# Last attention stage: another order of VectorE's work from the middle of a group

## The reference

```python
h = jnp.maximum(_layernorm(x, axis=-1), 0.0)
x = x + _L3_gnn_ref(h, adj, Wq, Wk, Wv, bv, Wo, bo)

# _L3_gnn_ref, 12 heads of 32
q = (x @ Wq.T).reshape(B, N, NUM_HEADS, HEAD)
k = (x @ Wk.T).reshape(B, N, NUM_HEADS, HEAD)
v = (x @ Wv.T + bv).reshape(B, N, NUM_HEADS, HEAD)
a = jnp.einsum('bnhd,bmhd->bhnm', q, k) * SCALE + encoding_bias[:, None, :, :]
pad_mask = jnp.all(a == 0, axis=-1)
a = jnp.where(pad_mask[..., None], -jnp.inf, a)
a = jax.nn.softmax(a, axis=-1)
a = jnp.nan_to_num(a)
o = jnp.einsum('bhnm,bmhd->bnhd', a, v).reshape(B, N, HIDDEN)
return o @ Wo.T + bo
```

## Time and profile before

| what | value |
|---|---|
| median of three runs | 2923.13 us (2920.32 to 2926.05) |
| the profiled execution | 2924.59 us, its span 2922.8 us |
| PE busy | 2767.9 us, 95% of the span |
| DVE busy | 1962.4 us, 67% |
| ACT busy | 1035.7 us, 35% |
| POOL busy | 961.9 us, 33% |
| mean granted clock of TensorE | 0.991 |
| L675 (PE, a projection by rows) | 1103.7 us busy, 60.4 us idle before it |
| chain that ended last | PE 72%, DVE 15%, issue 6%, POOL 4%, ACT 2% |

### The profile page before, as it was taken

How to read it: one execution, slowest core, us unless ns; L and a number is a source line. 1 busy time by engine, 2 the same in 40 slices (tenths; PEclk the granted TensorE clock), 3 DMA queues, 4 the chain that set the end, 5 groups by cost and what they waited for, 6 DMA issues and landing times.

```text
span 2922.8 us, 64340 instructions
## 1 busy us (share of the span) xinstructions
PE 2767.9 (95%) x26048; PEld 2337.1 (80%) x26048; DVE 1962.4 (67%) x4550; ACT 1035.7 (35%) x1985; POOL 961.9 (33%) x874
## 2 busy tenths in 40 slices
PE   6999999999989999999999999999998899999997
PEld 5888888888878888887888888888887777877776
DVE  4455445555567677778777776777777777777775
ACT  2333333333334444444333332222222344433342
POOL 1222113444443333333111110334344344444443
PEclk9999999999999999999999999999999999999999
DMA  3222332333421211221222223222332111111101
GB/s 95 69 69 76 100 106 83 99 109 109 128 70 36 72 48 49 72 73 57 71 71 71 61 88 111 70 92 81 103 103 86 37 36 49 48 48 48 36 26 36
DMA packets 197320, 211.45 MB, mean 72 GB/s; under 512 B 72736, under 2 KB 197024, under 8 KB 197024
## 3 DMA queue, kind: packets, MB, share of 16 engines
q1 hardware_dynamic: 197024, 207.33, 23.1%
HBM read 131.80 MB, written 75.50 MB: 71 GB/s over the span
## 4 chain that ended last, share of the span: by engine, by line
PE 72%; DVE 15%; issue 6%; POOL 4%; ACT 2%; DMA 1%; SPq 0%; DVEq 0%; POOLq 0%; ACTq 0%
PE psum L672 27%; PE psum L675 25%; DVE v_x L1504 4%; PE psum L723 3%; PE psum L990 3%; PE psum L660 2%; PE psum L840 2%; PE psum L885 2%; PE psum L829 2%; DVE room L1535 2%; PE psum L975 2%; PE psum L739 2%; POOL room L507 1%; POOL room L505 1%; PE psum L861 1%
## 5 line engine op out<-in xcount | busy, mean ns | idle before, releaser
L675 PE MATMUL psum<-fast 128*128 128x384 f32 x5760 | 1103.7, 343 | 60.4 <-DVE v_x L1504 28.1
L675 PEld LDWEIGHTS psum<-fast 128*128 128x128 f32 x5760 | 994.7, 189 | 129.6 <-DVE v_x L1504 39.3
L672 PE MATMUL psum<-fast 128*128 128x512 f32 x3456 | 861.7, 400 | 11.4 <-ACT room L1191 4.9
L672 PEld LDWEIGHTS psum<-fast 128*128 128x128 f32 x3456 | 637.1, 189 | 166.8 <-issue 22.7
L526 POOL TENSOR_TENSOR room<-room 128x768 f32<-128x768 f32 x128 | 188.8, 1475 | 418.4 <-DVE room L1541 260.2
L1642 DVE TENSOR_TENSOR room<-psum,rows 128x384 f32<-128x384 f32 x384 | 212.2, 553 | 120.4 <-PE psum L675 119.8
L1135 ACT ACTIVATE room<-psum 128x512 f32<-128x512 f32 x192 | 114.7, 597 | 391.3 <-PE psum L672 391.3
L660 PE MATMUL psum<-mask,z_sb 128*128 128x128 f32 x1152 | 177.7, 285 | 55.1 <-ACT z_sb L1116 21.9
L1116 ACT ACTIVATE z_sb<-x_ring,negb,rstd 128x384 f32<-128x384 f32 x256 | 168.0, 701 | 119.4 <-DVE negb L1367 119.4
L1504 DVE TENSOR_TENSOR v_x<-psum,rows 64x192 f32<-64x192 f32 x512 | 181.4, 354 | 27.9 <-PE psum L675 22.6
L660 PEld LDWEIGHTS psum<-mask,z_sb 128*128 128x128 f32 x1152 | 130.4, 143 | 85.9 <-issue 32.7
(11 more groups left out here) (96 smaller groups left out, 3575.0 us busy)
## 6 DMA issues: line engine op xcount, KB each, us to landing
x_ring<-x_mid SPq DMA_DIRECT2D x64, 768.0 KB, 4.6
x_mid<-x_ring SPq DMA_DIRECT2D x48, 768.0 KB, 4.0
x_ring<-x_in SPq DMA_DIRECT2D x32, 768.0 KB, 4.7
z_mid<-x_ring SPq DMA_DIRECT2D x32, 768.0 KB, 4.1
z_sb<-z_mid SPq DMA_DIRECT2D x32, 768.0 KB, 6.5
out<-x_ring SPq DMA_DIRECT2D x16, 768.0 KB, 3.9
w_raw<-w_all SPq DMA_DIRECT2D x19, 576.0 KB, 7.1
adjc<-adj SPq DMA_DIRECT2D x64, 128.0 KB, 3.9
```

The costliest lines, as they stand in the source:

```text
L672: mm = nc.tensor.matmul(dst, wpart[s_][:, c, c_out * P:(c_out + 1) * P], hpart[:, c, 0:GT], start=(k == 0), stop=(k == 3 * C - 1))
L675: mm = nc.tensor.matmul(dst[:, 0:H], hpart[:, c, row:row + P], wpart[s_][:, c, :], start=(k == 0), stop=(k == 3 * C - 1))
```

## The change

In `a_body` on VectorE, from `nat(0)` on, the last stage (`g.third`) gets an order of its own. `a_add_x` t1 stands ahead of `a_sums` t3; the value copies `nat` t1, the output rows `a_keep_o` t2 and the low part `low` 2 stand ahead of the scores' bias and maxima of the next group's t0 (`a_soft(F, 0)`); `a_sums(F, 0)` goes behind `a_keep_o` t3, and `a_soft(F, 1)` behind `nat` t3. The other attention stage takes the `else` branch, which has its old order. No instruction is added or removed, and no other engine's list changes.

```diff
--- before.py
+++ after.py
@@ -1611,23 +1611,36 @@
                 next_w(F, X, 1)
                 low(0)
                 nat(0)
-                a_sums(g, 3)
-                a_add_x(g, 1)
-                low(1)
-                if F:
-                    a_soft(F, 0)
-                nat(1)
-                a_keep_o(g, 2)
-                low(2)
-                if F:
-                    a_sums(F, 0)
-                nat(2)
-                if F:
-                    a_soft(F, 1)
-                a_add_x(g, 2)
-                a_keep_o(g, 3)
-                nat(3)
-                a_add_x(g, 3)
+                if g.third:
+                    a_add_x(g, 1)
+                    a_sums(g, 3)
+                    low(1)
+                    nat(1)
+                    a_keep_o(g, 2)
+                    low(2)
+                    if F:
+                        a_soft(F, 0)
+                    nat(2)
+                    a_add_x(g, 2)
+                    a_keep_o(g, 3)
+                    if F:
+                        a_sums(F, 0)
+                    nat(3)
+                    if F:
+                        a_soft(F, 1)
+                    a_add_x(g, 3)
+                else:
+                    low(1)
+                    if F:
+                        a_soft(F, 0)
+                    nat(1)
+                    a_keep_o(g, 2)
+                    low(2)
+                    nat(2)
+                    if F:
+                        a_soft(F, 1)
+                    a_keep_o(g, 3)
+                    nat(3)
 
             def c_nat(G, i):
```

## The result

The changed kernel takes 2995.78 us (median of four runs, 2990.58 to 2996.69), the kernel before 2924.47 (four runs, 2920.32 to 2926.05). The ratio is 1.0241, with a 95% interval of 1.0229 to 1.0254: slower, by 71 us. The forecast was 2985, the range 2964 to 3006.

The account below looks back on a forecast made before the run. TensorE bounds the last stage and VectorE causes all its waits. First body 0.5, thirteen full bodies 53.3, fifteenth 2.7 and last 5.1 add 61.6 us to the profiled 2924.6: 2986, forecast 2985 us, range 2964 to 3006.

Parts of the forecast that it names:

- The waits at parts 7 and 8 go, a wait at mix t3 comes: TensorE, last stage: waits of 0.54 and 1.21 us go; late first scores bring 2.3 us at mix t3.
- The residual add of t3 waits for GpSimd behind the second scores: End of VectorE's body: second scores six microseconds late, VectorE idle 2.7 us before this add, TensorE's part 1 waits 2.4.
- The loop: Ring of steps from one `a_soft(F, 1)` to the next: 44.04 us against 39.92, 4.1 us more per full body.
- The smaller waits: TensorE's idle time besides part 1 and mix t3: about 1.4 us at turn t1, the rest at the next body's first turn.
- The clock: Rival: TensorE's clock falls in many bodies, 2.6 us each; 3019 us in all, 3002 in half of them; chance 0.12.
- The first body: First body the change meets in the last stage: costs 0.5 us net.
- the fifteenth: Body without statistics or norms: pays only part 1 (2.4) and its own mix (0.3), 2.7 us.
- The last body: VectorE starts 5.1 us late, had 0.95 of pause, sums of t3 stand 0.9 later: costs 5.1 us.
- only mix t3 changes hands: Rival: VectorE's pauses swallow the second scores' lateness, each body costs 0.5 us, 2931 us; chance 0.07.
- faster: Rival: TensorE loses waits at parts 7 and 8, nobody misses the scores; 24 us gained, 2899 us; chance 0.04.

Follow-up runs that it names:

- The new end alone: Kernel before with only the end of VectorE's order changed (sums of next t0 and second scores later), old middle kept: 2976.30 us, ratio 1.0193.
- The early bias: Changed kernel with GpSimd's output bias of t3 ahead of the next group's weighing and second subtraction: 2969.90 us, ratio 1.0169 to the kernel before.
- The filled kernel: Changed kernel with TensorE's scores of t2 made three times and out t2 twice, same results: 2983.76 us, ratio 1.0210 to the kernel before.
- the middle alone: VectorE's middle as changed, but second scores ahead of the sums, output rows and value copy of t3: 2938.05 us, ratio 1.0062 to the kernel before.
- the kernel with both cures: Changed kernel with GpSimd's early bias of t3 and ScalarE's copy of turn t3's second half ahead of the exponential: 2937.05 us, ratio 1.0057.
- the residual add of t1 first: Kernel before with only the residual add of t1 put ahead of the sums of t3: 2939.58 us, ratio 1.0060.

## Why the prediction was right

Point by point, by its own steps.

- *The waits at parts 7 and 8 go, a wait at mix t3 comes.* So it was: 2.17 us, forecast 2.3. That half alone costs 17 us; its body by the sum was 40.8 and is 41.04, and an estimated 0.3 of it is the clock's.
- *The residual add of t3 waits for GpSimd behind the second scores.* 2.60 us, forecast 2.7; part 1 waits 2.3 to 2.7, forecast 2.4. The new end alone costs 55 us. The early bias takes this wait away and gives 23 back.
- *The loop.* Its steps, forecast and then measured in the body of 2648.36: second scores to residual add 5.57, 5.54; to `negb` 7.38, 7.26; to turn t1 2.04, 1.91; to part 7 13.75, 13.80; to the value copy 1.89, 1.89; to the scores 2.70, 2.67; to mix t3 5.91, 5.85; to the output rows 1.50, 1.49; to the next second scores 3.30, 3.29. The sum is 44.04 against 43.70. No step is off by more than 0.13 us. This is one of the short bodies; the mean of the thirteen is 44.43, and the sum has no term for the difference.
- *The smaller waits* were mis-sized: turn t1 waits 0.7 to 1.0 us, I had 1.4, and the first turn up to 0.7, where I had some 0.3. They are what is left over on TensorE, and not terms of the sum.
- *The clock* was held a rival with 0.12. It is a part of the result. The thirteen bodies are 58.7 us longer where the forecast has 53.3; at the undisturbed 43.9 they would be 51.9 longer, so some 7 us of the 71 are the lower clock. I had priced it by half of the bodies at 2.6 each; it is two of three at 0.4 to 1.0. The matmuls of parts 6 to 9 and the mixes take 13.9 us more over the thirteen bodies, of which about half shows in the time; the other half fell, as far as can be told, where TensorE would have waited later anyway (the first turn's wait of 0.7 us is there only behind the short bodies). The filled kernel shows these microseconds going, with 8.4. The forecast took the clock as nothing in its sum, and only its range had room for it.
- *The first body* was forecast 0.5 and cost 1.1, the fifteenth 2.7 and 2.6.
- *The last body* was forecast 5.1 and cost 7.1. From 2960 to 2980 us the granted clock is 0.66. That the clock is the two microseconds was not tried by itself.
- *The offset of 2.6 us* ahead of the stage is not the change's, and no forecast from one profile could have it.

The forecast of 2985 is 11 us low: the clock is most of it, the offset and the last body most of the rest. But for the loop, which the sum has 0.1 us a body too long against a short body, the errors go one way, so no large one was hidden by another. (The range of 3.0 to 5.0 us a body gives 2970 to some 2996, not 2998, which changes nothing.) The rival "only mix t3 changes hands" (2931) is what the middle alone does (2938), and fell for the whole, because VectorE's pauses lie behind the steps that come late. The rival "faster" fell at its place, mix t3, as the 3.5 us of lateness say: the first scores start 4.56 us after part 7 (2681.45 less 2676.89), as the forecast had it (2602.3 less 2597.7), and the wait of 2.17 us is there.

## What to carry to other kernels

When a step is moved back on one engine, look up what stands behind its successors in the queues of the others. Here the engine that waited was cured of 1.75 us, and a residual add and a copy that had nothing to do with the moved step stood behind it on GpSimd and ScalarE; add up the ring that is closed by this before counting the waits that go. A cure gives back only as far as the next link of the ring (1.5 of 2.7 us in the shortest bodies), and an order of one engine is good or bad only together with those of the others.

## What the hardware showed that was not expected

- Two waits of TensorE of 0.54 and 1.21 us in a body leave the granted clock at 1.00 from 2400 to 2800 us, and so do the waits of up to 1.6 us in the kernel with both cures; joined to one of 2.16 us, the first two bring it to 0.97 over that stretch and cost 0.8 us in ten of thirteen bodies. Some 1.2 to 1.7 us of repeated matmuls inside such a wait bring it back to 1.00, and the kernel gets faster by computing more: its last stage by 10.2 us in one case, by 9.9 in the other. In the first of them the repeated matmuls are transposes, and they kept the clock up too.
- Whether the clock falls in a body is not settled by the wait alone. In the changed kernel it falls behind mix t3 in two bodies of three, and this wait is 2.1 to 2.2 us in all; with the residual add of t1 first it falls in ten of thirteen, all with 2.16; with the middle as changed in all of them, with 2.17; and a single wait of 3.07 us left it at 1.00. What decides it was not tried.
